# Loading the stacked query and key parts of a batch in twelve transfers instead of thirty-six

## The chip, the core and the metric

The kernel runs on one core of a Trainium2 chip. The core has four compute engines that matter here: TensorE (PE), VectorE (DVE), ScalarE (ACT) and GpSimd (POOL). A fifth, SyncE (SP), computes nothing in this kernel; its instruction queue issues most of the DMA transfers. Each engine works through its own list of instructions in order, and engines wait for one another, and for transfers, through semaphores. The metric is the time of one execution on the device, in microseconds (us). The kernel before takes 697.2 us in the median of three runs (699.34, 697.2 and 695.61).

## The reference, cut to what matters

Four batches of 549 tokens (36 image patches and a class token, then 512 text tokens) of width 192 pass through one layer: layer norm, attention with 12 heads of 16 channels and a second softmax over 64 memory rows, and a mixture of 8 experts of which each token uses 2.

```python
h = tokens(x, W, b, class_token) + pos_embedding           # 4 x 37 x 192
h = concatenate([h, txt], axis=1)                          # 4 x 549 x 192
y = layernorm(h)
q, k, v = split_heads(y @ w_qkv + b_qkv)                   # 12 heads of 16
local = softmax(q @ k.T / 4) @ v                           # within a batch
mem   = softmax(q @ m.T / 4) @ m                           # m = memory @ w_mem + b_mem, 64 rows
h = h + (local + mem) @ w_out + b_out
h = h + moe(layernorm(h))                                  # router, top 2 of 8 experts, gelu
```

## The kernel before, in words

**Three bf16 parts.** The scores are computed to nearly fp32 accuracy from bf16 operands. Each value of q and k is split into three bf16 parts (high, middle, low), and the products of six pairs of parts are summed by one matmul whose contraction runs over 6 x 16 = 96 rows: `qst` holds the query parts 0,0,0,1,1,2 and `kst` the key parts 0,1,2,0,1,0, stacked in 16-row blocks, for 12 heads, with 549 and 640 columns (`Q_PARTS`, `K_PARTS`). Rows 96 to 99 carry an offset: the negated row maximum of the scores, in bf16 parts, so that the exponential needs no further subtraction.

**How a batch gets into `qst` and `kst`.** For batch b the parts are transposed on TensorE and copied by ScalarE into `partsT` (the `stack` stages). One transfer (`swap`, L600) writes them to a DRAM tensor `parts_transposed`. From there the `load` stages (L601 to L613) read them back into the 16-row blocks. There are three `load` stages for a batch, one for each group of four heads, and each issues 12 transfers: six blocks of `qst`, then six of `kst`. Each transfer writes 16 partitions, each with four rows (one for each head) of 549 or 640 bf16 values. Each head group has a semaphore, `s_load[j]`. `qst` and `kst` exist twice (`b % 2`).

**How attention runs.** There are 12 groups g (4 batches x 3 head groups). For each g, TensorE computes the `max` products (23 jobs, L982), VectorE takes their maxima, `negmax` forms the offsets, `maxT` transposes them (L994), ScalarE copies them to `mrow` (L815), and SP issues four small transfers (L620) from `mrow` to rows 96 to 99 of `qst`. Then come the 15 `score` jobs (L1011, four matmuls each) with their exponentials on ScalarE, and the 15 `value` jobs (L1026). The maxima of one group are computed among the scores of the group before. The first `max` job of a group waits for the loads of its group (L969); the first `score` job of a group waits for the four `mrow` transfers (`s_moff`).

**What sets the order.** `plan()` (L284 to L355) makes one list, `ORDER`, of all stages before the engine programs are built. It has several streams with due times, a table of which stage needs which (`needs`), and a small cost table for each engine (`Clocks.issue`), and takes at each step the stage that would leave TensorE idle least, weighed with its due time. Every engine's program then walks through the same list and takes out its own stages, so that list is also the order in each engine's queue. TensorE therefore does nothing of a later stage while it waits in an earlier one. The three `load` stages of a batch follow each other directly. In the list of the kernel before, the first `max` job of the next batch stands some thirty stages behind them, and the `maxT` of the group before stands a few stages behind that `max` job: around batch 1 the list reads load(1,0), load(1,1), load(1,2), ..., negmax(2), max(3,0,0), max(3,0,1), score(23), value(20), value(21), maxT(2), ..., score(30).

Of the kernel before, what the change touches and what calls it, by code (L numbers as in the profile page):

```python
# [39 lines left out]
B = 4  # L40
D = 192
DL = D - P
H, HD = 12, 16
# [9 lines left out]
GH = 4  # L53
G = H // GH
# [50 lines left out]
LEAD = 16  # L105
PHASE = 0.42
# [24 lines left out]
def needs(s):  # L131

    kind, i = s[0], s[1]
    batch = G * NC * TT
    if kind == "ln1":
        return [("refined", 0 if i < TT else 1)]
    if kind == "xT":
        return [("ln1", i)]
    if kind == "qk":
        return [("xT", i)] + ([("split", i - 2, 0)] if i >= 2 else [])  # L140
    if kind == "v":
        return [("xT", i)] + ([("value", (i // TT - 1) * batch - 1)] if i >= 2 * TT else [])
    if kind == "split":
        return [("split", i, 0)] if s[2] else [("qk", i)] + ([("turned", i - 2, 1)] if i >= 2 else [])
    if kind == "stack":
        return [("split", i, 1)] + ([("swapped", i // TT - 1)] if i % TT == 0 and i else [])
    if kind == "swap":
        return [("stack", i * TT + TT - 1, 1)]
    if kind == "load":
        return [("swapped", i)] + ([("score", (i - 1) * batch - 1)] if i >= 2 else [])  # L150
    if kind == "first":
        return [("moments", NT - 1)]
    if kind == "max":
        return [("loaded", i)]
    if kind == "negmax":
        return [("max", i, TT - 1, 2)] + ([("maxT", i - 2)] if i >= 2 else [])
    if kind == "maxT":
        return [("negmax", i)]
    if kind == "score":
        return (([("exp", i - 2)] if i >= 2 else []) + ([("value", i - PB)] if i >= PB else []) +  # L160
                ([("offset", i // (NC * TT))] if i % (NC * TT) == 0 else []))
    if kind == "value":
        return [("exp", i)] + ([("keep", i // TT - 1)] if i % TT == 0 and i else [])
    if kind == "keep":
        b = i // (G * NC)
        return [("value", i * TT + TT - 1)] + ([("att", (b - 1) * TT - 1)] if b >= 2 else [])
    if kind == "norm":
        return [("keep", (i // TT + 1) * G * NC - 1)] + ([("turned", i - 2)] if i >= 2 and s[2] else [])
    if kind == "whi" and i == 0:
        return [("value", (B - 1) * batch - 1), ("load", B - 1, G - 1)]  # L170
    before = {"attT": "att", "proj": "attT", "ln2": "rstd", "ln2T": "ln2", "router": "ln2T"}
    if kind == "rstd":
        return [("proj", i * TT + TT - 1)]
    if kind == "ln2":
        return [("rstd", i // TT)]
    return [(before[kind], i)] if kind in before else []


class Clocks:
# [32 lines left out]
    def issue(self, s):  # L212

        kind, i, at, on = s[0], s[1], self.at, self.on
        when, end, done = self.ready(s), None, None
        if span(s) is not None:
            ring = kind not in ("score", "value")
            if ring:
                slot = self.jobs % R
                self.jobs += 1  # L220
                when = max(when, self.free[slot])
            end = on("PE", span(s) + (MODE if (kind == "value") != self.columns else 0.0), when) + LAG
            self.columns = kind == "value"
            at[s] = end
        if kind == "img":
            done = on("DVE", 0.4, end)
        elif kind == "moments":
            at[s] = on("DVE", 0.55)
        elif kind == "first":
            a = on("ACT", 3.2, on("DVE", 0.25))  # L230
            at[("refined", 1)] = on("DVE", 0.9, a)
        elif kind in ("ln1", "ln2"):
            at[s] = on("DVE", 0.4, when) + 0.05
            if kind == "ln2":
                on("SP", 1.4, at[s])
        elif kind in ("xT", "attT", "ln2T"):
            at[("turned", i)] = end
            done = on("ACT", 0.45, end)
            at[s] = done + 0.1
        elif kind in ("qk", "v"):  # L240
            done = at[s] = on("ACT", 0.49 if kind == "qk" else 0.38, end)
        elif kind == "split":
            at[s] = (on("DVE", 0.95, when) if i < TT else on("POOL", 1.8, when)) + 0.08
        elif kind == "stack":
            at[("turned", i, s[2])] = end
            done = at[s] = on("ACT", (0.82, 0.5)[s[2]], max(end, when))
        elif kind == "swap":
            at[s] = on("SP", 0.4, when)
            at[("swapped", i)] = at[s] + 5.0
        elif kind == "load":  # L250
            at[s] = on("SP", 5.5, when)
            at[("loaded", i * G + s[2])] = at[s] + 2.3
        elif kind == "max":
            done = on("DVE", 0.61 if s[2] < TT - 1 or s[3] < 2 else 0.4, end) + 0.05
        elif kind == "negmax":
            at[s] = on("DVE", 0.66, when) + 0.08
        elif kind == "maxT":
            done = on("ACT", 1.25, end)
            at[("offset", i)] = on("SP", 2.5, done + 0.1) + 2.1
        elif kind == "score":  # L260
            at[("exp", i)] = on("ACT", 0.73, max(end, at.get(("value", i - PB), 0.0))) + 0.08
        elif kind == "keep":
            at[s] = on("ACT", 0.47, when) + 0.08
        elif kind == "norm":
            done = on("DVE", 0.6, end)
            if s[2]:
                at[("att", i)] = on("DVE", 0.38) + 0.05
        elif kind == "proj":
            done = on("DVE", 0.36, end) + 0.05
            at[s] = on("DVE", 0.65)  # L270
        elif kind == "rstd":
            at[s] = on("DVE", 0.9, on("ACT", 3.2, on("DVE", 0.25)))
        elif kind == "router":
            done = on("DVE", 0.2, end)
        elif kind == "whi":
            on("ACT", 1.46)
        elif kind == "wload":
            on("SP", 0.5)
        if done is not None and span(s) is not None and kind not in ("score", "value"):
            self.free[slot] = done  # L280
        at.setdefault(s, when)


def plan():  # L284
# [16 lines left out]
    units, NG = TT * NC, B * G  # L301
    scores, values, images, maxes, rest, loads, weights = streams = [[] for _ in range(7)]
# [24 lines left out]
    for b in range(B):  # L327
        at = b * G * units
        if b + 1 < B:
            spread(rest, front(b + 1), at, at + units * (1 + PHASE) - LEAD)  # L330
            loads += [(at + units * (1 + PHASE) - LEAD + 3.0 * j, ("load", b + 1, j)) for j in range(G)]
        if b > 0:
            spread(rest, merge(b - 1) + gate(b - 1), at + (units * (1 + PHASE) - LEAD if b + 1 < B else 0), at + G * units)
    w = list(range(EARLY))
# [7 lines left out]
    while any(h < len(x) for h, x in zip(head, streams)):  # L342
# [4 lines left out]
        _, _, n, s = min(choice)  # L347
# [29 lines left out]
def build(nc, a, out):  # L377
    ctx = ExitStack()
    sb = lambda name, shape, dt=F32: ctx.enter_context(nc.sbuf_tensor(name, shape, dt))
    sem = lambda name: ctx.enter_context(nc.semaphore(name))  # L380
    with ctx:
# [66 lines left out]
        at = sb("at", [P, HOTS, SLOT_TILES])  # L448
# [64 lines left out]
        s_koff, s_koffst = sem("s_koff"), sem("s_koff_placed")  # L513
        s_swap = sem("s_swap_stored")
        s_load = [sem(f"s_stacked_group{j}") for j in range(G)]
        s_neg = sem("s_neg")
        s_mrow = sem("s_mrow")
        s_moff = sem("s_moff")
# [46 lines left out]
        def _(sp):  # L565
# [29 lines left out]
            for s in ORDER:  # L595
                if s[0] == "swap":

                    b = s[1]
                    drained(sp, ("stack", b * TT + TT - 1, 1, 0))
                    sp.dma_start(swap[b].rearrange("(c p) s t -> p c s t", p=P), partsT[:]).then_inc(s_swap, 16)  # L600
                elif s[0] == "load":  # L601

                    _, b, j = s
                    sp.wait_ge(s_swap, 16 * (b + 1))
                    if b >= 2:
                        sp.wait_ge(s_score, (b - 1) * G * NC * TT)
                    if b >= 1:
                        sp.wait_ge(s_load[j], 16 * 2 * 6 * b)
                    for dst, row0, cols, which in ((qst, 0, T, Q_PARTS), (kst, D, KEYS, K_PARTS)):
                        heads = slice(j * GH, (j + 1) * GH)  # L610
                        src = swap[b, row0:row0 + D].rearrange("(h d) s t -> d h s t", d=HD)
                        for k, part in enumerate(which):
                            sp.dma_start(dst[b % 2][k * HD:(k + 1) * HD, heads, :],  # L613
                                         src[:, heads, part, 0:cols]).then_inc(s_load[j], 16)
                elif s[0] == "maxT":

                    g = s[1]
# [4 lines left out]
                elif s[0] == "ln2":  # L622

                    i = s[1]
                    b, t = divmod(i, TT)
# [6 lines left out]
                elif s[0] == "wload":  # L632
# [8 lines left out]
                    else:  # L641
                        src = a["w1"][0:P, c:c + n] if w == "w1a" else a["w2"][:, c:c + n]
# [255 lines left out]
        def _(pe):  # L898
# [43 lines left out]
            for s in ORDER:  # L942
                kind = s[0]
                if JOBS.get(kind):
                    i = s[1]
# [18 lines left out]
                elif kind == "max":  # L964
                    _, g, t, j = s
                    n, sl = rows_of(t), g // G % 2
                    if t == 0 and j == 0:

                        pe.wait_ge(s_load[g % G], 16 * 2 * 6 * (g // G + 1))  # L969
                    job_free(pe, s + (0,))  # L970

                    if t < TT - 1 and j < GH:
# [12 lines left out]
                elif kind == "maxT":  # L985
                    g = s[1]
# [531 lines left out]
```

## Time and profile before

| what | value |
|---|---|
| median of three runs | 697.2 us |
| profiled execution, its own time | 700.95 us |
| its span, first to last instruction | 698.7 us |
| mean granted TensorE clock | 0.882 of full |
| TensorE matmul busy | 583.5 us, 84% |
| VectorE busy | 426.5 us, 61% |
| ScalarE busy | 346.5 us, 50% |
| GpSimd busy | 210.1 us, 30% |

The page of the profile gives for each engine the busy time and, in 40 slices of 17.5 us, the busy share in tenths; below them stand the granted TensorE clock and the share of time in which the 16 DMA engines had packets in work. The span falls into a start until about 110 us (tokens, first batch), attention until about 410 us, routing until about 494 us, and the experts until the end. A line of the timeline reads: start, duration, engine, source line, operation, output and input tensor, sizes, how often, and in square brackets how long the engine had been idle before it and who released it. "SPq" is the issuing of transfers by SP.

### The profile page before, as it was taken

To read this page: it belongs to the slowest core of one execution; us is meant where nothing else is said; L and a number is where in the kernel's file an instruction comes from. 1 tells how busy PE (TensorE), PEld (TensorE's weight loads), DVE (VectorE), ACT (ScalarE), POOL (GpSimd) and SP (SyncE) were. 2 spreads that over 40 slices of the span, in tenths; PEclk is the share of its full clock that TensorE was granted. 3 is DMA by queue.
4 is the path that set the end of the run, shared out by engine and by line. 5 is a ranking of instruction groups with operands and counts; after the bars stand their busy time and mean duration, and the time that the engine had idled before them with its cause. 6 is when DMAs were issued, how large, how long until landed. Compare 5 with 4: busy or idle time off the path is not lost.

```text
span 698.7 us, 14697 instructions
## 1 busy us (share of the span) xinstructions
PE 583.5 (84%) x5165; PEld 432.3 (62%) x5166; DVE 426.5 (61%) x966; ACT 346.5 (50%) x664; POOL 210.1 (30%) x204
## 2 busy tenths in 40 slices
PE   3776999989999999999999784304599999999992
PEld 1541365556666566665666563203499999999992
DVE  2467727755498553887687256799255555555551
ACT  2440167657666747567467854330144444444441
POOL 3000141003400016000022444471245555555542
PEclk9795599989999889999999986555699999999997
DMA  7039003500072100440310354340123333333321
GB/s 234 3 114 130 2 1 112 136 3 1 3 184 62 42 17 2 143 104 28 123 27 25 110 125 128 113 135 0 31 46 51 56 51 52 54 50 53 53 39 17
DMA packets 35163, 46.47 MB, mean 67 GB/s; under 512 B 7860, under 2 KB 29861, under 8 KB 35114
## 3 DMA queue, kind: packets, MB, share of 16 engines
q1 hardware_dynamic: 26720, 35.10, 19.1%
q0 software_dynamic: 8064, 9.64, 8.6%
q10 hardware_dynamic: 330, 1.07, 0.4%
q8 instruction: 32, 0.52, 0.3%
q14 instruction: 17, 0.14, 0.1%
HBM read 31.26 MB, written 14.19 MB: 65 GB/s over the span
## 4 chain that ended last, share of the span: by engine, by line
PE 61%; DVE 13%; SPq 9%; DMA 7%; ACT 5%; issue 4%; POOL 0%; ACTq 0%; DVEq 0%; POOLq 0%
PE rings L901 12%; PE psS L901 10%; PE psO L1123 9%; PE psO L1026 7%; SPq L613 6%; PE psS L1011 6%; PE rings L982 6%; PE rings L1109 4%; DMA parts_transposed<-partsT 2%; DVE mx L1260 2%; DMA out<-yb,row 2%; PE rings L1041 1%; SPq L620 1%; PE rings L906 1%; PE rings L933 1%
## 5 line engine op out<-in xcount | busy, mean ns | idle before, releaser
L824 ACT ACTIVATE pr<-psS 128x732 f32<-128x732 f32 x180 | 137.2, 782 | 63.5 <-PE psS L1011 61.5
L1260 DVE TENSOR_REDUCE mx<-rings 128x1 f32<-128x512 f32 x192 | 124.0, 682 | 52.6 <-PE rings L982 51.8
L982 PE MATMUL rings<-kst,qst 96*128 96x512 bf16 (+3 forms) x480 | 108.7, 330 | 13.4 <-DMA kst<-parts_transposed 11.2
L1011 PE MATMUL psS<-qst,kst 100*128 100x183 bf16 x720 | 88.3, 251 | 3.8 <-DMA qst<-mrow 3.5
L729 POOL DMA_INDIRECT out<-yb,row x42 | 66.4, 1582 | 69.7 <-ACT yb L877 56.4
L1026 PE MATMUL psO<-pr,val 128*32 128x183 f32 x1440 | 80.7, 336 | 3.1 <-ACT oT L832 2.7
L1123 PE MATMUL psO<-w,hTh 128*128 x252 | 80.9, 370 | 1.3 <-DVE hTl L1426 1.3
L1011 PEld LDWEIGHTS psS<-qst,kst 100*128 100x128 bf16 x720 | 59.8, 101 | 26.4 <-issue 8.1
L677 POOL CAST qk_parts<-qk 128x384 bf16<-128x384 f32 (+1 forms) x15 | 7.5, 501 | 222.5 <-ACT qk L795 143.9
L871 ACT ACTIVATE hTh<-rings 128x384 fp32r<-128x384 f32 x84 | 36.6, 489 | 75.9 <-PE rings L1109 75.9
L982 PEld LDWEIGHTS rings<-kst,qst 96*128 96x128 bf16 (+1 forms) x480 | 35.8, 102 | 52.9 <-DVE mx L1260 18.0
L865 ACT ACTIVATE hg<-psS 128x768 f32<-128x768 f32 x42 | 34.2, 814 | 52.8 <-PE psS L901 52.8
L1123 PE MATMUL psO<-w,hTl 128*128 x252 | 57.5, 255 | 0.0
L1026 PEld LDWEIGHTS psO<-pr,val 128*32 128x32 f32 x1440 | 37.0, 111 | 29.4 <-issue 13.8
L1426 DVE TENSOR_TENSOR hTl<-rings,hTh 128x384 fp32r<-128x384 f32 x84 | 42.9, 552 | 18.5 <-ACT hTh L871 18.5
L708 POOL DMA_INDIRECT mx_in<-normalised,row x42 | 41.5, 989 | 40.6 <-DVEq L1412 20.2
L1123 PEld LDWEIGHTS psO<-w,hTh 128*128 128x128 f32 x252 | 47.5, 188 | 1.5 <-issue 1.5
L1123 PEld LDWEIGHTS psO<-w,hTl 128*128 128x128 f32 x252 | 47.5, 191 | 0.0
L702 POOL TENSOR_TENSOR w1a_low<-stage,w1a_high 128x512 fp32r<-128x512 f32 x12 | 15.0, 1278 | 105.6 <-ACT w1a_high L858 105.6
L746 ACT ACTIVATE xT_a<-rings 128x128 f32<-128x128 f32 (+1 forms) x60 | 15.9, 265 | 60.5 <-PE rings L907 60.1
L1262 DVE TENSOR_REDUCE mt<-rings 128x8 f32<-128x512 f32 x48 | 32.7, 682 | 19.6 <-PE rings L982 19.4
L1074 PE MATMUL psO<-sel,hot 128*128 128x126 f32 x40 | 9.6, 422 | 32.6 <-DVEq L1404 32.6
(174 smaller groups left out, 1140.6 us busy)
## 6 DMA issues: line engine op xcount, KB each, us to landing
stage<-in_w SPq DMA_DIRECT2D x10, 768.0 KB, 4.3
parts_transposed<-partsT SPq DMA_DIRECT2D x4, 1440.0 KB, 5.1
kst<-parts_transposed SPq DMA_DIRECT2D x72, 80.0 KB, 3.0
qst<-parts_transposed SPq DMA_DIRECT2D x72, 68.6 KB, 2.7
stage<-in_w SPq DMA_DIRECT2D x8, 384.0 KB, 5.4
rows<-in_txt SPq DMA_DIRECT2D x4, 384.0 KB, 7.3
out<-rows SPq DMA_DIRECT2D x16, 96.0 KB
normalised<-rows SPq DMA_DIRECT2D x16, 96.0 KB
```

Of the source, the lines that this page charges most:

```text
L613: sp.dma_start(dst[b % 2][k * HD:(k + 1) * HD, heads, :], src[:, heads, part, 0:cols]).then_inc(s_load[j], 16)
L708: pool.indirect_dma_start(out=mx_in[:, i % 2, :], out_offset=None, in_=xrow, in_offset=bass.IndirectOffsetOnAxis(ap=row[:, i:i + 1], axis= ...
L729: pool.indirect_dma_start(out=out, out_offset=bass.IndirectOffsetOnAxis(ap=row[:, i:i + 1], axis=0), in_=yb[:, i % 2, :], in_offset=None, ...
L824: act.activation(pr[:, n % PB], psS[:, n % 2, :, 0:2 * QC], ACT.Exp, scale=HD ** -0.5).then_inc(s_exp, 1)
L871: act.activation(hTh[:, cur, half * W:(half + 1) * W], ring[1 + half][:, 0:W], ACT.Copy).then_inc(s_hThi, 1)
L901: ins = pe.matmul(dst, l, r, start=(n == 0), stop=(n == len(pairs) - 1), **kw)
L982: ins = pe.matmul(bank(s + (0,))[r:r + n, c:c + k1 - k0], qst[sl][0:KQ, h, t * P:t * P + n], kst[sl][0:KQ, h, k0:k1], start=True, stop=True)
L1011: ins = pe.matmul(psS[:, n % 2, j // 2, (j % 2) * QC:(j % 2 + 1) * QC], kst[sl][0:KM, h, k * P:(k + 1) * P], qst[sl][0:KM, h, c * QC:(c + ...
L1026: ins = pe.matmul(psO[32 * j:32 * j + VW, 0:QC], val[sl][:, k, h, :], rhs, start=(k == 0), stop=(k == TT - 1))
L1123: ins = pe.matmul(*x, start=(c == 0 and x is wide), stop=(c == FC - 1 and x is wide))
L1260: ins = dve.tensor_reduce(mx[0:n, g % 2, t, j:j + 1], bank(s + (0,))[0:n, :], AX, ALU.max)
L1426: dve.tensor_tensor(hTl[:, cur, cols], ring[1 + half][:, 0:W], hTh[:, cur, cols], ALU.subtract).then_inc(s_hT, 1)
```

## The change

For batches 1 to 3 there is one `load` stage in place of three. It issues 12 transfers, and each moves all twelve heads of its 16-row block, three times as many bytes as before. All of them count on one new semaphore, `s_all`. Batch 0 keeps its three `load` stages and their semaphores. The first `max` job of each of the groups 3 to 11 waits for the twelve transfers of its whole batch. In the planner's tables, the one `load` costs SP the same 5.5 as one of the three did, makes all three groups available 2.6 later (before: 2.3), and `whi(0)` needs that one `load` instead of the last of three.

```diff
-        return [("value", (B - 1) * batch - 1), ("load", B - 1, G - 1)]
+        return [("value", (B - 1) * batch - 1), ("load", B - 1, 0)]
...
             at[s] = on("SP", 5.5, when)
-            at[("loaded", i * G + s[2])] = at[s] + 2.3
+            for j in range(G) if i else (s[2],):
+                at[("loaded", i * G + j)] = at[s] + 2.6
...
-            loads += [(at + units * (1 + PHASE) - LEAD + 3.0 * j, ("load", b + 1, j)) for j in range(G)]
+            loads.append((at + units * (1 + PHASE) - LEAD, ("load", b + 1, 0)))
...
+        s_all = sem("s_stacked_batch")
...
                     sp.wait_ge(s_swap, 16 * (b + 1))
                     if b >= 2:
                         sp.wait_ge(s_score, (b - 1) * G * NC * TT)
-                    if b >= 1:
-                        sp.wait_ge(s_load[j], 16 * 2 * 6 * b)
+                        sp.wait_ge(s_all, 16 * 2 * 6 * (b - 1))
                     for dst, row0, cols, which in ((qst, 0, T, Q_PARTS), (kst, D, KEYS, K_PARTS)):
-                        heads = slice(j * GH, (j + 1) * GH)
+                        heads = slice(j * GH, (j + 1) * GH) if b == 0 else slice(0, H)
                         src = swap[b, row0:row0 + D].rearrange("(h d) s t -> d h s t", d=HD)
                         for k, part in enumerate(which):
                             sp.dma_start(dst[b % 2][k * HD:(k + 1) * HD, heads, :],
-                                         src[:, heads, part, 0:cols]).then_inc(s_load[j], 16)
+                                         src[:, heads, part, 0:cols]).then_inc(s_load[j] if b == 0 else s_all, 16)
...
-                        pe.wait_ge(s_load[g % G], 16 * 2 * 6 * (g // G + 1))
+                        pe.wait_ge(s_load[g], 16 * 2 * 6) if g < G else pe.wait_ge(s_all, 16 * 2 * 6 * (g // G))
```

## Rows read from the trace of the kernel before

**Rows 1.** Page: slices of TensorE, granted clock, DMA; chain that ended last, by engine.
```profile
PE   3776999989999999999999784304599999999992
PEclk9795599989999889999999986555699999999997
DMA  7039003500072100440310354340123333333321
PE 61%; DVE 13%; SPq 9%; DMA 7%; ACT 5%; issue 4%; POOL 0%; ACTq 0%; DVEq 0%; POOLq 0%
```
**Rows 2.** Chain of waits, 100 to 150 us: start, duration, what.
```profile
109.85 0.63 ACT mrow L815
...
113.02 5.11 DMA parts_transposed<-partsT
...
140.25 1.70 DMA qst<-mrow
```
**Rows 3.** Timeline of SP around the loads of batch 1.
```profile
118.15 3.02 SPq L613 DMA_DIRECT2D qst<-parts_transposed  x6
121.21 3.04 SPq L613 DMA_DIRECT2D kst<-parts_transposed  x6
...
138.34 2.48 SPq L620 DMA_DIRECT2D qst<-mrow  x4
```
**Rows 4.** Timeline of TensorE in the same stretch.
```profile
126.87 0.60 PE L982 MATMUL rings<-kst,qst 96*128 96x512 bf16 x2 [0.80 <-DMA kst<-parts_transposed]
128.37 0.51 PE L994 MATMUL rings<-identb,mp 128*8 128x128 bf16 x10
139.10 0.39 PE L982 MATMUL rings<-kst,qst 96*128 96x512 bf16 x1 [0.21 <-DVE mt L1262]
141.99 1.41 PE L1011 MATMUL psS<-qst,kst 100*128 100x183 bf16 x8 [2.50 <-DMA qst<-mrow]
```
**Rows 5.** Timeline of SP: first loads of batches 0, 2 and 3.
```profile
48.24 2.69 SPq L613 DMA_DIRECT2D qst<-parts_transposed  x6
...
196.34 3.69 SPq L613 DMA_DIRECT2D qst<-parts_transposed  x6
...
289.48 2.67 SPq L613 DMA_DIRECT2D qst<-parts_transposed  x6
```
**Rows 6.** TensorE: last `max` job of group 5, first of groups 6 and 9.
```profile
208.39 0.30 PE L982 MATMUL rings<-kst,qst 96*37 96x128 bf16 x4
...
209.38 0.38 PE L982 MATMUL rings<-kst,qst 96*128 96x512 bf16 x1
...
301.83 0.38 PE L982 MATMUL rings<-kst,qst 96*128 96x512 bf16 x1
```
**Rows 7.** Page, part 6: issues by tensor: count, KB each, us from issue to landing.
```profile
kst<-parts_transposed SPq DMA_DIRECT2D x72, 80.0 KB, 3.0
qst<-parts_transposed SPq DMA_DIRECT2D x72, 68.6 KB, 2.7
```
**Rows 8.** Line L613, landings: issues of 48:54, then of 63:66 us (batch 0).
```profile
DMA to landing us min/median/max: 2.3/2.7/3.3
...
L613 SPq DMA_DIRECT2D kst<-parts_transposed x5: 426/426/427, 62.7 to 64.6; - x5
DMA to landing us min/median/max: 4.6/4.8/4.9
```
**Rows 9.** Windows: us, busy of five engines, PEclk, DMA share, GB/s.
```profile
54.00:66.00 12.00, 7.92 (x22) 2.12 (x22) 7.46 (x14) 0.43 (x2) 0.00 (x0) 0.50 1.11 142
68.00:69.00 1.00, 1.00 (x6) 0.45 (x5) 1.00 (x3) 0.00 (x0) 0.00 (x0) 0.50 0.04 3
121.20:124.30 3.10, 3.10 (x49) 1.86 (x42) 3.10 (x7) 2.06 (x3) 0.00 (x0) 1.00 0.63 161
```
**Rows 10.** Windows: only `kst<-koffb` in flight, a four-partition destination.
```profile
16.30:18.80 2.50, 0.00 (x0) 0.00 (x0) 0.67 (x3) 2.46 (x4) 0.00 (x0) 0.85 0.22 27
```
**Rows 11.** Windows: TensorE's clock after the wait that ended at 141.99.
```profile
142.00:150.00 8.00, 8.00 (x85) 5.32 (x85) 3.15 (x7) 4.47 (x6) 0.00 (x0) 0.64 0.00 0
```

## The prediction

> **What bounds the kernel now.** I read the slices and the chain by engine first [rows 1]. TensorE is busy nine tenths or more in nearly every slice between the first batch and the routing, and it holds 61% of the chain. So in the attention stage, where the change acts, each microsecond that TensorE loses is lost to the end, and each one that it is spared is gained. The same row gives SP's issuing 9% and DMA 7%, so the loads are on the path somewhere. The chain of waits around batch 1 shows where [rows 2, 3]. The swap to DRAM starts at 113.02 and takes 5.11 us; SP then issues 36 loads from 118.15 until 138.3; only then can it issue the four `mrow` transfers of group 2, the last of which takes 1.70 us to land, and TensorE starts its next scores at 141.99.
>
> TensorE's own timeline has two waits there [rows 4]. The first `max` job of group 3 starts at 126.87, 0.80 us late, released by the loads of the first head group; the first scores of group 2 start 2.50 us late, released by `mrow`. The second also cost clock: from 142 to 150 the granted clock averages 0.64 [rows 11]. At two levels, full and half, that is (1 - 0.64)/0.5 = 72% of 8 us, or 5.8 us, at half pace (1.2 GHz), so 2.9 us of work lost. In batches 2 and 3 the timeline shows no wait where the next batch begins. The place is found so [rows 6]: the narrow `max` products (96*37, 96x128) close group 5, and the next wide one, at 209.38, opens group 6 with no idle before it. Group 9 opens at 301.83. The loads of these batches began at 196.34 and 289.48 [rows 5]. So TensorE comes for a new batch 126.87 - 0.80 - 118.15 = 7.9, then 13.0, then 12.4 us after the first load is issued. Today it needs a third of the batch by then; after the change it needs the whole.
>
> **The issue side: what is removed.** 24 of 36 issues go in each of three batches. A row of six takes about 2.8 to 3.1 us [rows 3], so SP is busy some 5.6 us in place of 20. SP is free for `mrow` long before TensorE wants it, unless the queue holds it back. Either way `maxT(2)` comes behind `max(3,0,0)` in TensorE's list and cannot start while that waits. After its release the `mrow` chain takes 1.5 us of TensorE's work (126.87 to 128.37 [rows 4]), twice 0.63 on ScalarE and 2.48 and 1.70 for issue and landing [rows 2, 3]: 7 us, where TensorE has work until 139.5, 12.6 us after the release. The 2.50 us wait goes and nothing takes its place. Bounds: minus 2.5, and minus 2.9 more if no other wait drops the clock.
>
> **The data side: what is added.** The bytes stay: 18 x (80.0 + 68.6) KB a batch [rows 7], 2.74 MB. The question is how long they take when nothing paces them, and the nearest place is batch 0, the only one in which the 36 issues ran without a pause. There the landing time grew from 2.3 us for the earliest to 4.9 us for the last [rows 8], while the DMA share stood at 1.11 and the rate at 142 GB/s [rows 9]. 36 issues from 48.24 [rows 5] to 64.6 are one in 0.47 us, or about 160 GB/s, and the transfers did not keep up. From the first issue to the last landing (64.6 + 4.8) it took 21.2 us, and a microsecond earlier the engines had gone quiet [rows 9]. The 161 GB/s of batch 1 at a share of 0.63 [rows 9] lasts only between pauses in the issue. So the present stream runs close to the rate that this pattern sustains, and leaving out issues does not bring the last byte sooner.
>
> Bigger pieces could be faster or slower. From below: if the share of 0.63 at 161 GB/s could be filled, 161/0.63 = 256 GB/s, 10.7 us, and with the fixed 2.2 us of a landing 12.9 us. From above: a transfer into four partitions runs at 27 GB/s [rows 10]. If each four partitions take no more than that, one 16-partition transfer takes 4 x 27 = 108 GB/s, and the batch 25.4 + 2.2 = 27.6 us. Batch 0's 142 GB/s lies above 108 if two successive transfers, which write different 16-row blocks, overlap at their ends. With four rows per partition the ends are a large part of a transfer, with twelve a smaller one, so I expect a rate between the two. I take 23 us from first issue to last landing, nearer to batch 0's 21.2 than to 27.6.
>
> The Trainium skill speaks on both sides here. Its page "DMA: Bandwidth & Descriptors", section "Rules for kernel authors", advises to coalesce many small transfers into a large one; by that rule alone the change pays, as in the first rival below. Its page "SBUF — State Buffer", section "Door 1: The DMA port swizzle", says that 4 partitions share a port and that partitions 0 to 15 reach 4 of 16 ports, with 104 GB/s measured at 1 MiB; by that the batch would be an estimated 26 us of data, slightly beyond the third rival. The row agrees with its figure for one port (27 against 27.6 GB/s) [rows 10]; batch 0's 142 lies above its figure for four [rows 9].
>
> **The sum**, against the profiled execution (700.95 us; span 698.7, the rest lies around it). TensorE's list is strict, so the first `max` job of a batch waits for all twelve heads, with scores behind it that could run.
> - Batch 1: loads complete at 118.15 + 23 = 141.15, group 3 opens then and not at 126.87: +14.3. The 2.50 us wait goes: +11.8. The clock drops once before and once after: 0.
> - Batch 2: 196.34 + 23 = 219.34 against 209.38: +10.0, and a clock drop that was not there, priced as before [rows 11]: +2.9. Together +12.9.
> - Batch 3: 289.48 + 23 = 312.48 against 301.83: +10.7 + 2.9 = +13.6.
>
> Planner and waits: the new `load` promises its data 5.5 + 2.6 = 8.1 after it starts, the first of the three promised 7.8, so the list has no reason to put `max(3,0,0)` later, though the SP time freed in its table may shift single jobs. The dropped wait on `s_load` was met long before and costs nothing; the new one on `s_all` likewise. The wait of the first `max` job is the one priced above. Behind it stand all scores and values, and so ScalarE and the later maxima. What follows attention moves as a whole.
>
> Sum: 11.8 + 12.9 + 13.6 = 38.3 us. On the profiled execution 739; on the median 697.2 it is about 735. The median lies 3.7 us under the profiled execution, and I carry that difference over.
>
> **Rivals.**
> - *Issue-bound loads (faster).* If the twelve land as fast as they are issued, the batch is there after 5.6 + 2.3 = 7.9 us, just when TensorE asks in batch 1 and before it asks in 2 and 3. Gains: 0.8 + 2.5 + 2.9 = 6.2 us, so 691. For it: pauses aside, batch 1's windows show a DMA share of only 0.63. Against it: 2.74 MB in 7.9 us is 350 GB/s, and batch 0 fell behind at 142. It decides when the batch takes less than about 11 us.
> - *256 GB/s (same).* Complete after 12.9 us: batch 1 131.05, +4.2 - 2.5; batch 2 0; batch 3 +0.5. About +2, 699. Against it the same row of batch 0.
> - *Four-partition limit in full (more slowly still).* 27.6 us each: 4.6 us more in each batch, +13.8 on the sum: +52, 749. For it the four-partition row [rows 10]; against it the 142 GB/s.
>
> **Chances.** Forecast (rate of 120 to 142 GB/s, 723 to 743): 0.60. Full limit: 0.20. Between 256 and 142 GB/s (702 to 723): 0.05. Same: 0.05. Faster: 0.10. This kernel's measurement can't tell less than about 0.5% (3.5 us) from no change. Faster 0.10, same 0.05, slower 0.85. The range 708 to 751 leaves out the two upper rivals and little at the top.
>
> **What would show it.** In the new trace: 12 issues for each batch; the DMA share near 1 for some 20 us after the swap at 100 to 140 GB/s, and landings of up to 20 us; TensorE idle 10 to 15 us before the first `max` products of groups 3, 6 and 9, released by `kst`; a clock of 0.5 after each; no 2.50 us wait for `mrow` in batch 1. I am wrong if the landings of the last load come under 13 us after the first issue: then there is no stall and the time is at or below today's. I am wrong in size only if TensorE waits but the planner has put the group elsewhere.

## The result: 6.4% slower, and the profile after

The changed kernel takes 740.8 us in the median of four runs (736.84 to 746.38), the kernel before 696.4 us beside it: a ratio of 1.0641 (95% interval 1.0595 to 1.0688). The forecast was 735 us with a range of 708 to 751. The profiled executions are 737.65 us (span 735.5) against 700.95 (698.7), so the two traces hold 36.7 us of a difference that is 44.4 us between the medians: the one before lies above all four runs of its kernel (692.24 to 699.34), the one after at the lower end of its own. The other 7.7 us are not in these traces.

The page after, the rows that answer to those of before [rows 1]:

```profile
PE   3858998299992999967999988500589999999993
PEclk9795599599995999987999978655589999999997
DMA  7048007700097010292031153522013333333322
PE 50%; DMA 21%; DVE 13%; ACT 6%; SPq 5%; issue 4%; POOL 0%; ACTq 0%; DVEq 0%; POOLq 0%
```

TensorE has three holes in attention (2 in slice 8, 2 in slice 13, 6 and 7 in slices 18 and 19), and there the DMA row has its sevens and nines. In the chain DMA has 21% where it had 7%, SP 5% where it had 9%, and TensorE's share fell from 61% to 50%. Not all of that is the loads: by tensor the page gives 9% to `kst<-parts_transposed`, but also 8% to the output rows of the experts (`out<-yb,row`), which had 2% before. Those lie on another path through the last stage and are no part of the loss explained here.

SP around batch 1 (start, duration, how many) and TensorE where groups 3, 6 and 9 begin [rows 3, 4, 6]:

```profile
118.20 3.01 SPq L614 DMA_DIRECT2D qst<-parts_transposed  x6
121.27 3.28 SPq L614 DMA_DIRECT2D kst<-parts_transposed  x6
146.69 2.48 SPq L621 DMA_DIRECT2D qst<-mrow  x4
```
```profile
143.03 0.61 PE L983 MATMUL rings<-kst,qst 96*128 96x512 bf16 x1 [16.88 <-DMA kst<-parts_transposed]
...
233.94 0.61 PE L983 MATMUL rings<-kst,qst 96*128 96x512 bf16 x1 [13.01 <-DMA kst<-parts_transposed]
...
336.23 0.61 PE L983 MATMUL rings<-kst,qst 96*128 96x512 bf16 x1 [12.59 <-DMA kst<-parts_transposed]
```

SP is done after 6.3 us where it took 20, and TensorE then waits 16.88, 13.01 and 12.59 us for the last of the twelve transfers. The first issues of batches 2 and 3 are at 207.73 and 311.12, so the batch is complete 24.8, 26.2 and 25.1 us after its first issue. The landings of one batch and the windows of all three tell how [rows 8, 9]; the issue-to-landing row is that of the twelve transfers of batch 3:

```profile
L614 SPq DMA_DIRECT2D kst<-parts_transposed x6: 438/489/536, 313.9 to 316.5; - x6
DMA to landing us min/median/max: 4.2/12.1/19.7
```
```profile
120.00:141.00 21.00, 6.15 (x85) 3.58 (x83) 6.04 (x13) 5.15 (x9) 0.00 (x0) 0.74 1.11 121
210.00:232.00 22.00, 10.93 (x132) 6.97 (x124) 11.44 (x28) 6.36 (x13) 0.00 (x0) 0.78 1.12 115
313.00:334.00 21.00, 10.64 (x124) 6.73 (x116) 11.22 (x27) 6.12 (x12) 0.00 (x0) 0.78 1.12 120
```

The DMA engines are full (share 1.11) at 115 to 121 GB/s, less than the 142 of batch 0 with small transfers [rows 9].

### The profile page after: what moved, and what is told of

It reads as the page before. It is cut to its first block, busy times and chain, and to the rows that moved or that the text cites. A ratio compares the mean times of both kernels' runs of the same rounds, so it can differ in the third digit from the quotient of the medians.

```text
span 735.5 us, 14618 instructions
## 1 busy us (share of the span) xinstructions
PE 581.3 (79%) x5165; PEld 431.0 (59%) x5166; DVE 426.9 (58%) x966; ACT 346.4 (47%) x664; POOL 210.0 (29%) x204
## 4 chain that ended last, share of the span: by engine, by line
PE 50%; DMA 21%; DVE 13%; ACT 6%; SPq 5%; issue 4%; POOL 0%; ACTq 0%; DVEq 0%; POOLq 0%
PE rings L902 10%; DMA kst<-parts_transposed 9%; DMA out<-yb,row 8%; PE psS L902 7%; PE psO L1027 6%; PE psS L1012 6%; PE psO L1124 6%; PE rings L983 6%; SPq L614 4%; DMA parts_transposed<-partsT 3%; PE rings L1110 2%; DVE mx L1261 2%; PE rings L907 1%; SPq L621 1%; PE rings L1042 1%
## 5 line engine op out<-in xcount | busy, mean ns | idle before, releaser
L872 ACT ACTIVATE hTh<-rings 128x384 fp32r<-128x384 f32 x84 | 36.7, 489 | 76.0 <-PE rings L1110 76.0
L1434 DVE COPY ysum<-psO 128x192 f32<-128x192 f32 x42 | 15.0, 358 | 35.6 <-PE psO L1124 35.6
```

The lines of the kernel that those rows point to most:

```text
L872: act.activation(hTh[:, cur, half * W:(half + 1) * W], ring[1 + half][:, 0:W], ACT.Copy).then_inc(s_hThi, 1)
```

## The experiments

My theory after the result: the sixteen neighbouring destination partitions of a transfer hold the rate, and TensorE loses time because it works its list strictly in order and waits there for all heads. The rivals: the size of a transfer by itself, a cost for each packet, the reading side, the single queue, and the list that the planner wrote anew. The line number of the loads is L613 to L616 in these kernels; the ratios are to the kernel before, timed beside each.

### Small transfers, one wait

```diff
-  one load: 12 transfers of 12 heads on s_all
+  one load: for jj in range(G): 12 transfers of heads jj*4 .. jj*4+3, all on s_all (36)
```


> The changed kernel's list and its single wait for the whole batch, but each transfer of batches 1 to 3 cut into three of four heads again, all on the one semaphore: 36 issues, one wait. Theory (the data, not the issue, is the limit, and TensorE waits for all heads): SP issues for some 20 us and the last lands 2 to 4 us later, 22 to 24 us after the first issue. TensorE waits some 14, 9 and 9 us before groups 3, 6 and 9, and the time is 725 to 735 us. Rival (large transfers are at fault): with small ones the time goes back to that of the kernel before, 694 to 700 us.

Measured: 729.1 us, ratio 1.0458 (1.0385 to 1.053). TensorE waits 13.27 us in batch 1, released 21.2 us after the first issue, and 8.79 and 8.05 us in batches 2 and 3:

```profile
140.12 0.61 PE L984 MATMUL rings<-kst,qst 96*128 96x512 bf16 x1 [13.27 <-DMA kst<-parts_transposed]
```

The rival is out: small transfers do not bring the time back. Most of the loss is the wait for all heads, and the large pieces add the rest (21.2 against 24.8 us).

### The list alone

```diff
-  .then_inc(s_load[j] if b == 0 else s_all, 16)
+  .then_inc(s_load[jj], 16)                      # 36 transfers, a semaphore for each group
-  pe.wait_ge(s_load[g], ...) if g < G else pe.wait_ge(s_all, ...)
+  pe.wait_ge(s_load[g % G], 16 * 2 * 6 * (g // G + 1))
```


> The changed kernel's list (one load stage in the planner for each batch), but with the 36 small transfers and a semaphore for each head group as before: what the reordered list does by itself. Theory (the list changes little, the loss is the wait for all heads behind a slow transfer): 694 to 702 us, with TensorE waiting under 1 us before group 3 and 2 to 4 us for mrow in batch 1. Rival (the reordering costs part of the loss): 705 us or more.

Measured: 699.3 us, ratio 1.0037 (1.0013 to 1.0062). With the list of the changed kernel and everything else as before, group 3 waits 0.53 us, but the scores of group 2 come to their wait earlier, and that grows from the 2.50 us of before to 5.92:

```profile
126.41 0.39 PE L985 MATMUL rings<-kst,qst 96*128 96x512 bf16 x1 [0.53 <-DMA kst<-parts_transposed]
141.07 0.79 PE L1014 MATMUL psS<-qst,kst 100*128 100x183 bf16 x4 [5.92 <-DMA qst<-mrow]
```

So the new list costs 1 to 4 us, and the single wait some 30 on top of it (1.0458 against 1.0037).

### Half the heads, and half of each row

```diff
-  heads = ... slice(0, H)
+  heads = ... slice(0, H if b == 1 else H // 2)          # first kernel
-  dst[...][..., heads, :]          <- src[:, heads, part, 0:cols]
+  dst[...][..., heads, 0:cols//2]  <- src[:, heads, part, 0:cols//2]   # second, b >= 2 (274 and 320 columns)
```


> The changed kernel, but in batches 2 and 3 the loads bring only heads 0 to 5 (the other heads keep older data, so their part of the output is left out): half the bytes and half the packets. All theories: the loads of those two batches take half the data time, 12.5 + 2 = 14 us after the first issue, the waits before groups 6 and 9 shrink from 13 to 1 to 3 us, and the clock drops go with them, 712 to 720 us.

> The changed kernel, but in batches 2 and 3 each row is loaded to half its length (274 and 320 columns of 549 and 640; the rest keeps older data and is left out of the result): half the bytes, all the packets. Theory (bytes into the destination are the limit): as with half the heads, 14 us and 712 to 720 us. Rival (each packet costs its DMA engine a fixed time): the loads still take about 25 us and the time stays at 735 to 741 us.

Measured: 709.8 and 711.7 us, one run each. The landings of batch 3, first with half the heads, then with half of each row:

```profile
L614 SPq DMA_DIRECT2D kst<-parts_transposed x6: 427/428/438, 299.1 to 301.4; - x6
DMA to landing us min/median/max: 2.9/5.0/7.0
```
```profile
L614 SPq DMA_DIRECT2D kst<-parts_transposed x6: 438/438/440, 301.2 to 303.7; - x6
DMA to landing us min/median/max: 3.1/5.6/7.7
```

From first issue (296.3 and 298.5) to last landing that is 12.1 and 12.9 us, against 25.1 with everything. Half the bytes in all the packets is nearly as quick as half the packets: the bytes are what is paid for, and a fixed cost of each packet as the limit is out. The waits before groups 6 and 9 are gone with half the heads; 0.27 and 0.38 us of them are left with half of each row. The two times came out 2.2 and 0.3 us below the foot of my range.

### Two queues, to different and to the same partitions

The query transfers go out from SP, the key transfers from ScalarE. The two kernels differ from one another in one list only:

```diff
+  act.wait_ge(s_swap, ...); ...
+  for k in (1, 0, 3, 2, 5, 4):      # apart; (0, 1, 2, 3, 4, 5) in the other kernel
+      act.dma_start(kst[b % 2][k * HD:(k + 1) * HD, :, :], src[:, :, K_PARTS[k], :]).then_inc(s_all, 16)
```


> The changed kernel, with the six query transfers of a batch issued by SP and the six key transfers by ScalarE, in an order in which the two in flight never write the same set of four-partition groups modulo 32 (query blocks 0,1,2,3,4,5, key blocks 1,0,3,2,5,4). Theory (the destination's 16 partitions hold one stream at about 115 GB/s): the two streams add up to 170 to 220 GB/s, the batch is complete 14 to 18 us after the first issue, the waits shrink to 7, 3 and 3 us, and the time is 705 to 718 us (ScalarE loses 3 us of issuing a batch). Rival A (a limit on the reading side or common to all transfers): 115 GB/s and 25 us as in the changed kernel, 737 us. Rival B (one queue is the limit, wherever it writes): fast here and just as fast in the next kernel.

> The same two queues, but query and key blocks in the same order (0,1,2,3,4,5 both), so that what is in flight goes to the same 16 partitions on both. Theory (destination): no gain from the second queue, 105 to 125 GB/s, complete 23 to 26 us after the first issue, 733 to 742 us. Rival B (one queue is the limit): as fast as with the blocks apart, 705 to 718 us. Rival A: 737 us in both.

Measured: 727.1 us (1.0429, 1.0348 to 1.0511) apart and 745.1 us (1.0688, 1.0603 to 1.0772) to the same partitions. Windows while the loads of batches 1 and 2 are under way, apart and then the same (the last two numbers are DMA share and GB/s):

```profile
120.00:137.00 17.00, 9.45 (x87) 4.93 (x84) 6.54 (x13) 5.88 (x9) 0.00 (x0) 0.72 1.07 157
205.00:222.00 17.00, 12.24 (x144) 7.80 (x142) 12.59 (x31) 6.78 (x13) 0.00 (x0) 0.93 1.08 148
```
```profile
122.00:144.00 22.00, 8.99 (x83) 4.87 (x83) 6.05 (x12) 5.87 (x9) 0.00 (x0) 0.66 1.11 117
213.00:234.00 21.00, 10.99 (x124) 6.82 (x116) 11.24 (x27) 6.78 (x13) 0.00 (x0) 0.86 1.12 111
```

A second queue gives nothing by itself (111 to 117 GB/s, as with one), and the order of the destination blocks gives a third (148 to 157). So neither one queue nor something common to all transfers sets the rate of the same-partition case. But I had expected 170 to 220 GB/s and 705 to 718 us; two queues into different partitions do not add up. Why not is open. With the blocks apart a batch was complete 19.9, 21.9 and 20.0 us after its first issue (expected: 14 to 18), and TensorE waited 6.67, 8.31 and 6.52 us (expected: 7, 3 and 3). The waits are also no full measure of the loss here: in batch 1, where ScalarE now spends 3.22 us issuing, TensorE comes to group 3 at 131.58 and not at 126.15.

### The same transfers to partitions six apart

```diff
-  dst[b % 2][k * HD:(k + 1) * HD, heads, :]
+  dst[b % 2][k:KQ:6, heads, :]
```


> The changed kernel with one edit: block k of the stacked parts is written to partitions k, k+6, ..., k+90 and not to 16k to 16k+15, for qst and kst alike and in all batches (the matmul sums over all 96 rows, so it computes the same). Sources, sizes, number and order of the transfers stay. Theory (the 16 neighbouring destination partitions hold the rate): the loads run at 200 to 350 GB/s and are complete 10 to 15 us after the first issue; TensorE waits 2 to 6 us before group 3 and not at all before 6 and 9, and the time is 692 to 704 us. Rival (the reading side, or a cost of each packet on its DMA engine): 110 to 120 GB/s and waits of 17, 13 and 13 us as before the edit, 741 us.

> The same one edit in the kernel before (36 small transfers a batch, a semaphore for each head group). Theory: in batch 0 the landing time no longer grows over the 36 issues, so it stays at 2.3 to 3 us where it rose to 4.9; batches 1 to 3 are paced by SP's issuing and stay as they are, 20 us for 36 issues. 1 to 3 us less in all, 693 to 696 us. Rival: nothing changes, 697 us, and the landings of batch 0 still grow to 4.9 us.

Measured on the changed kernel: 714.0 us, ratio 1.0252 (1.02 to 1.0303), that is 27 us less than without the edit. Its windows during the loads of batches 1 to 3:

```profile
124.00:136.00 12.00, 6.08 (x84) 3.59 (x83) 5.97 (x13) 5.08 (x8) 0.00 (x0) 0.91 1.05 223
203.00:216.00 13.00, 11.89 (x142) 7.59 (x140) 11.97 (x29) 6.89 (x13) 0.00 (x0) 1.00 1.08 208
298.00:311.00 13.00, 11.47 (x137) 7.36 (x136) 11.92 (x30) 6.89 (x13) 0.00 (x0) 1.00 1.04 209
```

Same sources, same sizes, same queue, same number of packets: 208 to 223 GB/s in place of 115 to 121. The destination's partitions held the rate; that is shown. The batches are complete after 15.2 (122.14 to 137.31), 16.0 and 15.7 us, past the 15 I had given, TensorE still waits 7.23, 2.81 and 3.21 us before groups 3, 6 and 9, and the time is 10 us above my range. One reason shows in the kernel before with the same edit. There I had expected 693 to 696 us and measured 723.2 us (1.0386, 1.0328 to 1.0445). Its SP, and two of TensorE's waits:

```profile
L613 SPq DMA_DIRECT2D kst<-parts_transposed x9: 595/595/599, 62.9 to 71.8; - x9
DMA to landing us min/median/max: 2.2/2.3/2.4
```
```profile
149.36 1.41 PE L1011 MATMUL psS<-qst,kst 100*128 100x183 bf16 x8 [4.08 <-DMA qst<-mrow]
...
328.62 0.79 PE L1011 MATMUL psS<-qst,kst 100*128 100x183 bf16 x4 [5.64 <-DMA qst<-mrow]
```

The landings of batch 0 no longer grow (2.4 us at most, where they reached 4.9), as foretold. But the issue of a transfer takes 595 ns on SP and not 426 [rows 8], so the 36 of batch 1 take 25 us, and the `mrow` transfers behind them come later still. I had priced this at nothing. In all, TensorE's waits for `mrow` grew from 3.5 to 15.0 us and those for `kst` from 11.2 to 15.2; the other 7 of the 22.4 us between the two spans I have not traced.

### Four heads, then eight

```diff
-  load(b, 0): heads 0 to 11
+  load(b, 0): heads 0 to 3 on s_load[0];  load(b, 1): heads 4 to 11 on s_all
```


> Group 0's heads in twelve transfers of four heads, then groups 1 and 2 together in twelve of eight heads: 24 issues a batch, group 0 on its own semaphore. Theory (the transfers are held by the destination, and mrow stands behind them in the same queue): the first head group lands 8 to 9 us after the first issue, so TensorE waits about 1 us before group 3; SP is free after 11 us, but mrow lands only when the whole batch has, 22 to 24 us after the first issue, and the scores wait for it 4 to 8 us in batch 1 and 0 to 3 in the others: 696 to 708 us. Rival (mrow was late only for SP's issuing): mrow lands 2 us after its issue, that wait is gone, 689 to 693 us.

Measured: 703.0 us, ratio 1.0106 (1.0039 to 1.0172). TensorE waits 1.08 us before group 3. The chain of waits then shows what an early issue is worth:

```profile
133.45 8.17 DMA qst<-mrow
141.62 0.05 issue
141.66 0.80 PE psS L1013 x4
```

The last `mrow` transfer, issued at 133.45, lands 8.17 us later, where it took 1.70 with an empty queue [rows 2]. It comes down half a microsecond after the last load ahead of it (issued at 131.1, landed 10.0 us later): it stands behind the loads, of which this window of the same kernel still sees the DMA engines full (share 1.02, 127 GB/s):

```profile
134.00:140.00 6.00, 2.03 (x29) 1.09 (x26) 2.85 (x5) 2.13 (x4) 0.00 (x0) 1.00 1.02 127
```

### The second and third load behind mrow

```diff
-  loads += [(at + units * (1 + PHASE) - LEAD + 3.0 * j, ("load", b + 1, j)) for j in range(G)]
+  loads += [(at + units * (1 + PHASE) - LEAD + (0.0, 21.0, 24.0)[j], ("load", b + 1, j)) for j in range(G)]
```


> The kernel before, with its three loads of a batch kept but the second and third due later, so that in SP's list the four mrow transfers of the group before stand ahead of them. Theory (in batch 1 the scores waited 2.50 us for mrow because SP was issuing, and lost 2.9 us more to the clock): mrow goes out at about 131, that wait and the clock drop at 142 are gone, the 0.80 us wait stays, and nothing else changes: 5 us less, about 691 us. Rival (the second group's loads, now later, come late for group 4 or mrow queues behind the first loads): no gain, 695 us or more.

Measured: 689.5 us, ratio 0.9901 (0.9865 to 0.9937), 1.5 us below what I had expected: a small gain but clear of the noise, and the fastest kernel of this case. SP, TensorE where group 3 begins, what the scores waited for, and a window with the clock (third number from the end):

```profile
128.47 2.48 SPq L620 DMA_DIRECT2D qst<-mrow  x4
131.05 2.73 SPq L613 DMA_DIRECT2D qst<-parts_transposed  x6
```
```profile
125.09 0.60 PE L982 MATMUL rings<-kst,qst 96*128 96x512 bf16 x2 [0.62 <-DMA kst<-parts_transposed]
```
```profile
  DMA qst<-mrow: 0.8, 2
```
```profile
138.00:146.00 8.00, 8.00 (x119) 5.13 (x117) 6.89 (x14) 5.78 (x10) 0.00 (x0) 1.00 0.61 133
```

The 2.50 us wait of before [rows 4] is gone (0.8 us in two waits is left of them all), and with it the clock drop [rows 11].

### And two queues in batch 0

```diff
+  # in ScalarE's program, at load(0, j):
+  act.wait_ge(s_swap, 16)
+  for k in (1, 0, 3, 2, 5, 4): act.dma_start(kst[0][...], ...).then_inc(s_load[j], 16)
```


> The kernel with the second and third load of a batch put behind mrow, and in batch 0, where TensorE stands idle for its first loads, the key transfers issued by ScalarE beside the query transfers by SP. Theory: the first head group is issued in 2.8 us and not 5.6 and held by the destination at 142 to 154 GB/s, so it is complete 7 us after the first issue and not 8.4; the later groups of the batch are no earlier. 1 to 3 us less than without this edit, 686 to 689 us. Rival (the rate alone decides): no gain.

Measured: 695.4 us, ratio 0.9969 (0.994 to 0.9999) against 0.9901 without this edit, so about 5 us worse and not 1 to 3 better. ScalarE reached its issues only at 52.20, behind an activation that ended at 52.16, where SP could begin at 49.37, and TensorE's first wait grew from 9.18 to 12.51 us:

```profile
52.20 1.29 ACTq L787 DMA_DIRECT2D kst<-parts_transposed  x3
```

That is 3.3 us; the rest of the loss I have not traced.

## Why the prediction was right, step by step

- **TensorE is the bound and its list is strict.** Right. The three waits grew, and no other wait of TensorE grew by more than half a microsecond.
- **The rate does not rise with fewer issues.** Right, and the reason given for it (the destination) is shown by the kernel with partitions six apart. Not shown is the finer picture of the sum, that each four partitions take 27 GB/s and that successive transfers overlap at their ends: 115 to 121 lies above 4 x 27 = 108, and no run varied the rows of a transfer with the issue out of the way. The rate also lies at or below the foot of the 120 to 142 that I had tied to my forecast, though the time lies within it. The two rules of the Trainium skill that were weighed point opposite ways, and the measurement sides with "SBUF — State Buffer", "Door 1: The DMA port swizzle" (104 GB/s for partitions 0 to 15, measured at 1 MiB; here, a little above it, 115 to 121 with successive blocks) against the advice to coalesce in "DMA: Bandwidth & Descriptors", "Rules for kernel authors".
- **23 us to the last landing.** Too short: 24.8, 26.2 and 25.1. The waits rose by 16.88 + 13.01 + 12.59 - 0.80 - 2.50 = 39.2 us, where the sum had 32.5 before its clock terms. This was the term of the sum that was sized too small.
- **The 2.50 us wait for `mrow` goes.** Right: the only wait for `mrow` left is one of 0.61 us at 374.94.
- **Two new clock drops of 2.9 us.** They came: after the waits the granted clock is 0.60 from 233 to 241 and 0.59 from 336 to 343. But in these two traces they were too much in the net, since the kernel before had two drops of its own in batch 2 that I had not looked for. They are the first two windows below; the third is the changed kernel behind its wait of batch 2, with the clock full throughout (third number from the end):

```profile
230.00:240.00 10.00, 8.57 (x76) 4.76 (x76) 4.93 (x15) 7.58 (x13) 0.00 (x0) 0.66 0.16 46
250.00:260.00 10.00, 10.00 (x63) 6.65 (x63) 4.39 (x11) 4.08 (x12) 1.39 (x2) 0.66 0.01 2
```
```profile
240.00:320.00 80.00, 77.30 (x863) 49.42 (x855) 54.66 (x123) 52.87 (x108) 14.12 (x20) 1.00 0.21 45
```

  Priced as in the prediction, each of the two cost 10 x (1 - 0.66) = 3.4 us of work, and the one after the wait of batch 2 cost 8 x (1 - 0.60) = 3.2. Idle and busy time of TensorE over batches 1 to 3 and the merge, before and then after:

```profile
118.15:196.34 78.19, 73.32 (x855) 46.13 (x848) 47.27 (x90) 50.95 (x94) 14.23 (x20) 0.96 0.20 56
196.34:289.48 93.14, 90.59 (x958) 57.34 (x956) 61.44 (x142) 58.30 (x117) 14.13 (x20) 0.93 0.23 58
289.48:412.00 122.52, 113.39 (x1399) 74.37 (x1398) 81.30 (x199) 85.36 (x150) 15.92 (x13) 0.97 0.29 79
```
```profile
118.20:207.73 89.53, 71.77 (x858) 45.49 (x848) 47.09 (x91) 50.88 (x94) 14.22 (x20) 0.90 0.32 49
207.73:311.12 103.39, 87.68 (x958) 55.27 (x956) 61.70 (x141) 58.06 (x117) 14.12 (x20) 0.92 0.33 52
311.12:449.00 137.88, 116.67 (x1399) 76.13 (x1398) 81.23 (x199) 85.29 (x150) 15.70 (x13) 0.90 0.35 70
```

  The stretches grow by 11.3, 10.3 and 15.4 us, 37 in all, and TensorE's busy time (the first number behind each length) does not grow: 277.3 before, 276.1 after. If the half clock had cost more than before, the same matmuls would have been busy longer. So the drops after the waits took the place of others. In these traces +38.3 was forecast and +36.7 came, which is partly luck, by errors of opposite sign: 6.7 us too little for the waits, 5.8 too much for the clock, and 2.5 us of small gains that I can't place.
- **Between the medians** it was +44.4, 6 us more than forecast, about what the waits were short of. The profiled execution of the kernel before is one of its slower ones, at a mean clock of 0.882; other executions near 694 us ran at 0.893. So it may have had more drops than most, and the forecast's 5.8 us for the clock may hold for the medians. Whether it does is open: no trace of a median execution was kept.
- **The list hardly changes.** Right in size (1 to 4 us, measured with the separate semaphores), though I had counted it as nothing; what it costs behind the larger waits was not measured. The planner was told 8.1 us where the loads took 25. No run gave it the measured time, so whether a list with the `max` jobs later would hide part of the waits stays open.
- **The rivals.** The issue-bound case needed 350 GB/s and met 115 to 121. The full four-partition limit (108 GB/s, 27.6 us) came slightly nearer to the measured 25.4 us than my 23 did; its time of 749 us lies further from the measured 740.8 than my 735.

## What to carry to other kernels

A transfer that carries all heads makes the first consumer wait for all of them: before merging transfers, find the wait that ends last at the first consumer and ask how much of the data it needs, and what rate the transfers reach when nothing paces their issue. The place to read that rate is where they ran back to back (DMA share above 1, landings that grow), not a mean over windows with pauses. And what is in SP's list ahead of a small urgent transfer delays it twice, by its issue and by its bytes in the queue; moving the urgent one ahead gained 1%, where merging lost 6%.

## What the runs showed of the hardware

- Twelve-row transfers ran at 115 to 121 GB/s into sixteen neighbouring partitions and at 208 to 223 into sixteen partitions six apart, with equal sources and packets. Four-row transfers into neighbouring ones reached 142 in batch 0; why more is not shown.
- Two queues with twelve-row transfers ran at 111 to 117 GB/s when both wrote the same blocks in the same order, and at 148 to 157 with the blocks apart.
- The issue of a four-row transfer on SP took 426 ns to neighbouring partitions and 595 ns to partitions six apart.
- A 4.3 KB transfer behind loads in the same queue took 8.17 us to land, and 1.70 with none ahead.
- Executions of the changed kernel spread over 1.3% (736.84 at a mean clock of 0.872 to 746.38 at 0.857); what the clock follows there was not settled.
